# Last block: the fourth pair of split parts of the last sum lies in the tiles' load buffers instead of a row buffer

## The reference, cut to what matters

```python
scores = softmax(x @ gate_weight.T)                 # 1024 rows, 16 experts
topk_weight, topk_idx = top_k(scores, 4)
for e in range(16):                                 # routed experts, 176 channels each
    w_e = sum(where(topk_idx == e, topk_weight, 0))
    y = y + w_e[:, None] * (silu(x @ G_e.T) * (x @ U_e.T) @ down_e.T)
y = y + silu(x @ G_s.T) * (x @ U_s.T) @ down_s.T    # shared expert, 352 channels
x = x + layernorm(y)
```

## Time and profile before

| | us |
|---|---|
| median of 3 runs | 1164.43 (1162.33 to 1166.17) |
| the profiled execution | 1165.97 |
| its span | 1164.2 |

### The profile page before, as it was taken

The page is one execution under the profiler, slowest core; times in us unless marked ns, Lnnn a source line. Parts: engine busy times, 40 slices in busy tenths (PEclk is TensorE's granted clock), DMA queues, the critical chain, the costliest instruction groups (busy, mean ns, idle before and its releaser), DMA issues. The chain is left out here.

```text
span 1164.2 us, 18668 instructions
## 1 busy us (share of the span) xinstructions
PE 1063.6 (91%) x6437; PEld 820.7 (70%) x6437; DVE 784.8 (67%) x1802; ACT 679.0 (58%) x1241; POOL 519.3 (45%) x491
## 2 busy tenths in 40 slices
PE   7999999979998968498999999999789999998797
PEld 5423322246887957388889889889789878887797
DVE  6888888646665643487899998998557455333443
ACT  4577777756543444476788778778445344332354
POOL 5361420013079231375667767776605100447234
PEclk9999999999998986699999999999889999999799
DMA  3221221115235001565556355532010123554100
GB/s 84 54 60 29 47 42 28 47 29 164 73 83 130 15 1 25 60 73 117 77 72 71 78 69 78 68 73 58 19 34 20 46 55 95 157 162 145 34 19 19
DMA packets 108886, 75.97 MB, mean 65 GB/s; under 512 B 29188, under 2 KB 100056, under 8 KB 108792
## 3 DMA queue, kind: packets, MB, share of 16 engines
q1 hardware_dynamic: 108496, 74.55, 31.1%
q10 hardware_dynamic: 296, 0.23, 0.1%
HBM read 65.51 MB, written 1.28 MB: 57 GB/s over the span
## 5 line engine op out<-in xcount | busy, mean ns | idle before, releaser
L700 DVE TENSOR_REDUCE attn_row_max<-attn_rows_q 128x1 f32<-128x512 f32 x256 | 159.0, 682 | 27.3 <-PE attn_rows_q L468 25.9
L603 ACT ACTIVATE attn_probs<-attn_rows_k 128x512 f32<-128x512 f32 x256 | 136.7, 602 | 42.6 <-PE attn_rows_k L478 42.4
L478 PE MATMUL attn_rows_k<-attn_q_stack,attn_k_stack 99*128 99x512 bf16 x256 | 95.3, 380 | 1.8 <-ACT attn_probs L603 1.7
L468 PE MATMUL attn_rows_q<-attn_k_stack,attn_q_stack 96*128 96x512 bf16 x256 | 95.8, 383 | 0.9 <-DMA attn_k_stack<-attn_part 0.5
L2690 DVE TENSOR_TENSOR late_mids<-late_mids,late_bank 128x512 f32<-128x512 f32 (+1 forms) x50 | 34.3, 687 | 77.5 <-PE late_bank L80 74.6
L78 PE MATMUL late_bank<-net_x_part_low,late_w_T 128*128 128x512 f32 (+1 forms) x192 | 77.9, 406 | 0.0
L468 PEld LDWEIGHTS attn_rows_q<-attn_k_stack,attn_q_stack 96*128 96x128 bf16 x256 | 24.7, 97 | 74.1 <-DVE attn_row_max L700 47.4
L79 PE MATMUL late_bank<-net_x_part_low,late_w_T 128*128 128x512 f32 (+1 forms) x192 | 76.1, 396 | 0.0
L80 PE MATMUL late_bank<-net_x_part_low,late_w_T 128*128 128x512 f32 (+1 forms) x192 | 76.0, 396 | 0.0
L1455 POOL TENSOR_TENSOR gold_mids<-gold_mids,gold_weight 128x512 f32<-128x512 f32 x32 | 51.6, 1651 | 46.2 <-DMA gold_weight<-gold_weights 44.9
L2595 ACT ACTIVATE late_mids<-late_bank 128x512 f32<-128x512 f32 (+1 forms) x50 | 29.8, 597 | 69.6 <-PE late_bank L80 69.6
(11 more groups left out here) (415 smaller groups left out, 3390.2 us busy)
## 6 DMA issues: line engine op xcount, KB each, us to landing
lin_mix<-decay_sums SPq DMA_DIRECT2D x16, 512.0 KB, 15.6
lin_q_dec<-decay_sums SPq DMA_DIRECT2D x16, 512.0 KB, 21.2
gold_weight<-gold_weights SPq DMA_DIRECT2D x16, 256.0 KB, 3.5
s_raw_ring<-in_L_ffn_Wg SPq DMA_DIRECT2D x12, 256.0 KB, 3.2
s_raw_ring<-in_L_ffn_Wu SPq DMA_DIRECT2D x12, 256.0 KB, 3.9
gold_raw_w_down<-in_L_ffn_Wd SPq DMA_DIRECT2D x1, 2048.0 KB, 12.7
early_lin_w_q<-in_L_attn_Wq SPq DMA_DIRECT2D x16, 128.0 KB, 17.2
early_lin_w_k<-in_L_attn_Wk SPq DMA_DIRECT2D x16, 128.0 KB, 13.1
```

Source lines behind the costliest of these rows:

```text
L468: pe.matmul(ps_q[n % 3][:, :], q_stack[0:QROWS, h, r * P:(r + 1) * P], k_stack[0:QROWS, h, b * HALF:(b + 1) * HALF], start=True, stop=True ...
L478: pe.matmul(ps_k[n % 3][:, :], k_stack[0:QROWS + MROWS, h, t * P:(t + 1) * P], q_stack[0:QROWS + MROWS, h, b * HALF:(b + 1) * HALF], start ...
L603: act.activation(probs[:, kk % PB, b * HALF:(b + 1) * HALF], ps_k[n % 3][:, :], ACT.Exp)\
L700: dve.tensor_reduce(row_max[:, r, b:b + 1], ps_q[n % 3][:, :], axis=AX, op=ALU.max)\
```

## The change

The two load buffers become one tensor of the same size, over whose memory a second name of the parts' type (`natural_low`) is laid. The fourth pair of parts is its two halves, and no longer `w_T_last`. ACT's wait before unit 3 becomes `w_turned` of all 25 tiles (PE has transposed the last tile out of the load buffers) in the place of 42 weighings. The order of the instructions, their number and their shapes stay; the size of the memory too.

```diff
--- before.py
+++ after.py
@@ -2316,7 +2316,7 @@
         w_T = [s.sb(f"w_T{b}", [P, 2, 2, DK, P], F32R) for b in range(W_RING - 1)]
         raw_space, w_T_last = over(nc, s, "w_T_last", [P, 2, 2, DK, P])
         w_T.append(w_T_last)
-        natural = [s.sb(f"natural{b}", [P, 2, D]) for b in range(LOAD_RING)]
+        natural, natural_low = over(nc, s, "natural", [P, LOAD_RING, 2, D])
 
         row_space, down, gw_space, order_space = space
         weight = [raw_space[:, :, :, :, :].rearrange("p q m k f -> p (q m k f)"),
@@ -2325,7 +2325,8 @@
         w_o_high = down_T[0][:, ST + 1:ST + 1 + LH, :]
         flat = "p a d -> p (a d)"
         out_parts = [[down_T[1][:, at:at + 2, :].rearrange(flat) for at in (4 * b + 4, 4 * b + 6)] for b in range(W_RING)]
-        sum_parts = [[w_T[b][:, q, :, :, :].rearrange("p m k f -> p (m k f)") for q in range(2)] for b in range(W_RING)]
+        sum_parts = [[w_T[b][:, q, :, :, :].rearrange("p m k f -> p (m k f)") for q in range(2)] for b in range(W_RING - 1)]
+        sum_parts.append([natural_low[:, b, :, :].rearrange("p m d -> p (m d)") for b in range(2)])
         xn = mids[:, RT - 2:RT, :].rearrange("p a (c d) -> p (a c) d", d=D)
         scratch = [mids[:, b:b + 2, :].rearrange("p a (c i j) -> p (a c) i j", i=NX, j=NX) for b in (RT - 7, RT - 5)]
         scratch.append(mids[0:NX, RT - 3, :])
@@ -2408,7 +2409,7 @@
                         sp.wait_ge(w_turned, i - LOAD_RING + 1)
                         sp.wait_ge(d_turned, i - LOAD_RING + 1)
                     for what, rows, src in tile_loads(TILES[i], weights):
-                        dst = {"gate": natural[b][rows, 0, :], "up": natural[b][rows, 1, :], "down": down[b][:, :, rows]}[what]
+                        dst = {"gate": natural[rows, b, 0, :], "up": natural[rows, b, 1, :], "down": down[b][:, :, rows]}[what]
                         sp.dma_start(dst, src).then_inc(loaded[b], 16)
 
                 def load_rows(tile):
@@ -2478,7 +2479,7 @@
                         pe.wait_ge(w_split, i)
                     for m in range(2):
                         for k in range(DK):
-                            t = pe.transpose(ps_w[:, m, k, 0:rows], natural[b][0:rows, m, k * P:(k + 1) * P],
+                            t = pe.transpose(ps_w[:, m, k, 0:rows], natural[0:rows, b, m, k * P:(k + 1) * P],
                                              ident[0:rows, 0:rows])
                     t.then_inc(w_turned, 1)
                     if i >= 1:
@@ -2569,7 +2570,7 @@
                     if u < W_RING - 1:
                         act.wait_ge(up_done, AT[NTILE - W_RING + 1 + u, 1] + 1)
                     elif u < W_RING:
-                        act.wait_ge(weighted, 2 * RT - 2)
+                        act.wait_ge(w_turned, NTILE)
                     else:
                         act.wait_ge(sum_used, u - W_RING + 1)
                     if n < ST:
```

## The result

| | before | after |
|---|---|---|
| median of 6 runs, us | 1163.06 (1162.11 to 1166.17) | 1152.74 (1147.54 to 1156.60) |
| ratio of the runs | | 0.9908 (95%: 0.9880 to 0.9935) |
| profiled execution, us | 1165.97, span 1164.2 | 1155.43, span 1153.6 |
| last sum, first to last matmul | 1069.15 to 1157.33: 88.18 us | 1070.97 to 1146.71: 75.74 us |

The time fell by 10.7 us by the ratio (7.6 to 14.0 by its interval). Within the profiles it can be placed: the last sum is 12.44 us shorter, what follows it takes the same (6.87 us before, 6.89 after), and the last sum begins 1.82 us later. 1.6 us of this are there at the first matmul of the first layer's scores (29.1 us before and 30.7 after), long before anything that the change touches. 12.44 - 1.82 = 10.6, the difference of the spans.

What follows compares the result with a forecast made beforehand. PE was held before unit 3 by ACT's wait for a weighing, then restarted at a low clock: 13.72 us together. Less 1.4 given back, 12.3 us gained: median 1164.43 to 1152.1 us, range 1149 to 1156.

Steps and rivals of the forecast that it cites:

- The wait removed: Before unit 3: ACT's wait for weighing 42 goes, its replacement costs nothing, and PE's hole of 11.24 us closes.
- The slow restart: PE's low clock after the hole: 2.41 us lost at units 3 and 4, another 0.07 at units 5 and 6.
- What is given back: Early units: DVE's low parts run beside POOL's weighings, 1.68 us per cycle against PE's 1.44; loss 1.4 us.
- The extra turn of DVE: A POOL gap of over 0.55 us gives DVE one low part out of turn, so it is ahead again.
- the second of the two cases: The out-of-turn low part falls into POOL's gap before tile 20, not the gap of about 0.6 us before tile 19.
- The sum: Whole kernel: 13.72 - 1.4 = 12.3 us gained; profiled execution 1165.97 to 1153.7, median 1164.43 to 1152.1.
- Full recovery: POOL's row loads open more gaps, DVE never behind after unit 3: loss 0.2, gain 13.5, 1150.9 us; chance 0.14.
- Strict turns: DVE and POOL alternate with no extra turn, POOL bound by its rows: loss 2.9, gain 10.8, 1153.6 us; chance 0.12.
- whole instructions blocked: DVE and POOL each wait out the other's full length, cycle 1.93 us: gain 9.6, 1154.8 us; chance 0.05.
- The clock did not fall: Rival denied here: PE's clock drops once although fed at 86%, losing 2.5 us: gain 9.8, 1154.6 us; chance 0.05.

Runs made afterwards that it cites:

- the run with the old wait: Changed kernel with ACT's wait for 42 weighings before unit 3 put back, new place kept; ratio to the kernel before 0.9996, median 1162.69 us.
- the filled hole: Kernel before, with 46 matmuls put in PE's queue between units 2 and 3; last sum 85.60 us, median 1161.02 us, ratio 0.9968.
- the short weighings: Changed kernel, POOL weighing only 16 of 512 columns for routed tiles 18 to 21; last sum 74.38 us, median 1150.14 us, ratio to before 0.9886.
- the constants: Changed kernel, weighings of routed tiles 18 to 21 replaced by POOL writing a constant there; last sum 74.36 us, 1144.84 us in one run.
- the halves: Changed kernel, row buffers loaded and released in halves; last sum 74.39 us, 75.20 in a second profile; median 1150.59 us, ratio to before 0.9899.

## Why the prediction was right

- *The wait removed.* Right, by the run with the old wait: `w_turned` cost nothing, ACT's part 3 followed part 2 at once (1071.17 and 1071.71), and the hole of 11.24 us is down to 0.17.
- *The slow restart, 2.48 us.* Right for the profile that it was worked out from: 2.5 by the filled hole, and the granted clock after stays at 1.00. Other profiles with the old wait have 2.1 to 2.5.
- *What is given back, 1.4 us.* Measured 1.28 (75.74 against 74.46), or 1.36 against the short weighings' 74.38. By steps, from the start of the sum: unit 3 was foreseen at 4.57 us and came at 4.53; units 4 and 5 at 6.25 and 7.93, and came at 6.22 and 7.92. The extra turn of DVE fell before tile 20, as the second of the two cases had it. Off was what followed: the prediction had one extra turn in a gap of just over 0.55, and PE falling behind once more before the last weighing. The gap before tile 19 was 0.44 us and not 0.6, and gave no turn. The row of tile 20 landed 4.68 us after tile 18's end and not 4.26, so that gap was 1.26 us, DVE did three low parts in a row, and that was enough until the end. The loss came out alike, five waits at units 3 to 7 in the place of a few before and a few after the gap. POOL was through 19.4 us after the start of the sum, 2.6 later than before and not 1.4; nobody waited, as foreseen.
- *The sum.* 12.3 foreseen, 12.44 in the last sum. The profiled execution was to be 1153.7 and was 1155.43, by the 1.82 us of late start. The median, 1152.74, is 0.6 from the forecast. That both are so near is partly luck: the interval of the ratio is 6 us wide, and the hole itself varied by 2 us between profiles. With the second profiles of both kernels the last sum gains 13.06 (88.75 to 75.69).
- *The rivals.* Full recovery needed the weighings out of the way: it is what the short weighings, the constants and, in one profile, the halves gave. Strict turns and whole instructions blocked are out: the cycle was 1.70 us, and a gap did give extra turns. The clock did not fall with PE fed at 1.44 of 1.70.
- *The Trainium skill* ("SBUF — State Buffer", section "SBUF: two separate sides") says that the loser of the lock fully blocks. The traces agree that it waits for the other's end (1.77 beside a weighing). The constants agree with its section "Who interferes with whom", by which a GpSimd instruction that only writes doesn't contend with a DVE instruction of two SBUF inputs: 0.69. Adding the two durations alone (1.93) is what the measured cycle of 1.70 doesn't bear out.

What stays open: why the 42nd weighing, which waits for its row of weights, ends up to 2.7 us earlier in one execution than in another.

## What to carry to other kernels

When a ring's place is shared with something of another stage, look at what its first use waits for: here one wait on an engine with an in-order queue held everything behind it for 11 us, though its own work had been ready. Price such a hole with the slow clock behind it, and subtract what the work that used to fall into the hole will now cost beside it. Where the whole time scatters by more than the change, measure the stage in the profile, from its first to its last instruction.

## What the runs showed of the hardware that I had not expected

Most of the scatter of the whole time is there before the last layer's sum. In the twelve profiles the last sum began between 1061.84 and 1071.46 us. The first matmul of the first layer's scores differs by 1.9 us (28.8 to 30.8). For one and the same matmul of the third layer the spread is 2.6 us near 528 us in the span, and 6.5 near 556. It becomes 9.6 near 860, where the last layer begins. From there to the last sum it stays at 9.6.

The last of these steps can be seen in two windows that are laid over the same 120 matmuls, at the end of the third layer and the start of the last one. The first is of the second profile of before, the second of the one with constants (columns as in the earlier trace rows):

```profile
833.89:861.55 27.66, 21.08 (x121) 20.18 (x121) 11.39 (x18) 8.33 (x11) 6.23 (x3) 0.77 0.12 34
```

```profile
829.07:851.97 22.90, 16.31 (x122) 15.32 (x122) 10.20 (x17) 8.21 (x11) 6.22 (x3) 0.97 0.11 32
```

The same work took 27.66 us at a mean granted clock of 0.77, and 22.90 us at 0.97: 4.8 of the 9.6 us between these two profiles. Why the clock is lower there in one execution than in the other isn't shown.
